# Order of the moved columns, weight sums and operand splits in a fused conv and FFN kernel

## The reference, cut to what matters

```python
x = x + L0_ffn(L0_cond(x, cond_128, conv weight, c_weight, bias), W, b, A, B, gate_w, gate_b)
x = x + L1_ffn(L1_cond(x, cond_128, W0..W2, weight, bias_k), W_base, b_base, router, lora_A, lora_B)
# L0_cond: grouped 9-tap convolution along the 1024 axis, plus a per-channel term
# L1_cond: a 64 x 64 channel mixture drawn per sample from 8 weights, plus a bias
# L*_ffn : x @ W.T + b, plus a rank-limited product chosen by a gate
```

## Time and profile before

| | us |
|---|---|
| median of 3 runs | 504.15 (504.13 to 504.69) |
| the profiled execution | 504.05 |
| its span, first to last instruction | 502.3 |
| TensorE busy in it | 493.3 (98%) |
| VectorE, GpSimd, ScalarE busy | 355.2, 160.6, 141.2 |

### The profile page before, as it was taken

The page is one execution under the profiler, slowest core; times in us unless marked ns, Lnnn a source line. Parts: engine busy times, 40 slices in busy tenths (PEclk is TensorE's granted clock), DMA queues, the critical chain, the costliest instruction groups (busy, mean ns, idle before and its releaser), DMA issues.

```text
span 502.3 us, 8338 instructions
## 1 busy us (share of the span) xinstructions
PE 493.3 (98%) x2889; PEld 456.3 (91%) x2889; DVE 355.2 (71%) x781; ACT 141.2 (28%) x298; POOL 160.6 (32%) x134
## 2 busy tenths in 40 slices
PE   8999999999999999999998999999999999999997
PEld 8989999999989899898997989898998989889886
DVE  4966998557495885958879668686666657657654
ACT  4732334242324323243152322121112112111200
POOL 1000020022455524555004744350626225062620
PEclk9999999999999999999999999999999999999999
DMA  8945205438286583867799863332515232160312
GB/s 312 327 143 173 86 1 158 147 116 281 68 277 216 199 275 108 275 206 222 247 412 404 331 196 119 127 105 71 202 44 188 85 126 106 64 209 2 126 43 84
DMA packets 43653, 86.40 MB, mean 172 GB/s; under 512 B 4299, under 2 KB 19259, under 8 KB 43612
## 3 DMA queue, kind: packets, MB, share of 16 engines
q1 hardware_dynamic: 34556, 63.49, 37.7%
q10 hardware_dynamic: 9056, 22.38, 12.2%
HBM read 58.81 MB, written 24.97 MB: 167 GB/s over the span
## 4 chain that ended last, share of the span: by engine, by line
PE 51%; DVE 2%; issue 0%; DVEq 0%
PE b_p L1729 6%; PE b_x L1749 4%; PE b_x L1748 4%; PE b_x L1746 4%; PE b_p L1730 3%; PE b_m L1705 3%; PE b_y L1749 3%; PE b_y L1746 3%; PE b_y L1748 3%; PE b_z L1748 2%; PE b_z L1749 2%; PE b_z L1746 2%; PE b_w L1749 1%; PE b_w L1748 1%; PE b_w L1746 1%; PE b_y L1705 1%
## 5 line engine op out<-in xcount | busy, mean ns | idle before, releaser
L730 ACT CAST a_hi<-mixed 128x512 fp32r<-128x512 f32 x63 | 37.7, 620 | 152.3 <-DVE mixed L1110 80.5
L655 POOL TENSOR_TENSOR xs<-xs,mixw_sb 128x512 f32<-128x512 f32 x28 | 38.3, 1379 | 118.4 <-DMA xs<-x_scratch 83.7
L1729 PE MATMUL b_p<-wp,a_hi 128*128 128x464 f32 (+1 forms) x224 | 72.6, 377 | 0.0
L1730 PE MATMUL b_p<-wp,a_lo 128*128 128x232 f32 (+1 forms) x224 | 60.1, 268 | 0.0
L1146 DVE TENSOR_TENSOR a_lo<-mixed,a_hi 128x512 fp32r<-128x512 f32 x63 | 53.4, 881 | 4.1 <-ACT a_hi L730 3.8
L1307 DVE TENSOR_TENSOR xs<-b_x,xs 128x464 f32<-128x464 f32 (+2 forms) x52 | 33.4, 642 | 27.7 <-PE b_x L1789 15.6
L741 ACT CAST s_hi<-s_sums 128x512 fp32r<-128x512 f32 x56 | 34.1, 620 | 59.8 <-POOL s_sums L618 36.1
L1154 DVE TENSOR_TENSOR s_lo<-s_sums,s_hi 128x512 fp32r<-128x512 f32 x56 | 43.9, 818 | 9.1 <-POOL s_sums L623 9.1
L1729 PEld LDWEIGHTS b_p<-wp,a_hi 128*128 128x128 f32 x224 | 42.1, 188 | 5.1
L618 POOL TENSOR_TENSOR s_sums<-mixed 128x512 f32<-128x512 f32 x13 | 17.9, 1376 | 80.6 <-DVE mixed L1107 55.5
L1730 PEld LDWEIGHTS b_p<-wp,a_lo 128*128 128x128 f32 x224 | 42.8, 191 | 0.6
(11 more groups left out here) (310 smaller groups left out, 1272.5 us busy)
## 6 DMA issues: line engine op xcount, KB each, us to landing
blk<-x_scratch SPq DMA_DIRECT2D x16, 512.0 KB, 4.0
xs<-in_x SPq DMA_DIRECT2D x30, 256.0 KB, 3.4
x_scratch<-xs SPq DMA_DIRECT2D x30, 256.0 KB, 3.8
xs<-x_scratch SPq DMA_DIRECT2D x28, 256.0 KB, 2.9
out_dram<-xs SPq DMA_DIRECT2D x27, 256.0 KB, 2.3
blk<-in_xblk SPq DMA_DIRECT2D x10, 516.0 KB, 3.7
w_raw<-in_wcat SPq DMA_DIRECT2D x8, 546.0 KB, 8.6
praw<-in_wcat ACTq DMA_DIRECT2D x8, 464.0 KB, 4.8
```

Source lines behind the costliest of these rows:

```text
L655: pool.tensor_tensor(x_rows, x_rows, bbase[:, a:b], ALU.add).then_inc(x_biased[q], 1)
L730: act.copy(a_hi[:, op, :, :], mixed[:, op, :, :]).then_inc(ahi_done[op], 1)
L1729: pe.matmul(both, x_hi, wp[:, k, :, 0:PLAIN[l]], start=(k == 0), stop=False, skip_group_check=True)
L1730: ins = pe.matmul(dst, x_lo, wp_hi[:, k, 0:PLAIN[l]], start=False, stop=(k == NCH - 1), skip_group_check=True)
```

## The change

Five edits, all in the order of work. The instructions are the same and none is added.

1. SyncE (`shift_pair` part of its list): `move_z(a, 0)` is issued ahead of the waits for the stores of pair g-1 and the loads of regions 3 and 1, not after them.
2. GpSimd: in pairs 3 to 6 the two `add_z` stand ahead of `prep(g)`, not after it.
3. ScalarE, pairs 3 to 6: `split_a(A11)`, `split_a(A12)` of the next pair ahead of all four `prep_split`.
4. VectorE, pairs 3 to 6: `split_a(A11)` and `split_a(A12)` right behind `take_first`; P5 taken after `fin11`; `prep_split` of blocks 0, 1 and 3 ahead of taking P6; `split_s(S4)`, `prep_split(2)`, the second `sum_mix` and the taking of `b_w` after it; `take_plain(0)` then.
5. Pair 7: `split_plain` ahead of `load_slot(T1, P5)` on ScalarE and ahead of taking P5 on VectorE.

```diff
@@ SyncE, shift pairs @@
+                    move_z(a, 0)
                     stored(3, g - 1)
                     load_x(3, g)
                     stored(1, g - 1)
                     load_x(1, g)
-                    move_z(a, 0)
                     if shifted(a - 2):
                         stored(2, g - 1)
                         load_x(2, g)
@@ GpSimd @@
             for g in range(FULL, LAST + 1):
-                if PREP_FIRST <= g <= PREP_LAST:
-                    prep(g)
                 if shifted(2 * g + 2):
                     add_z(2 * g + 2, 0)
                     add_z(2 * g + 2, 1)
+                if PREP_FIRST <= g <= PREP_LAST:
+                    prep(g)
@@ ScalarE, shift_pair @@
-                prep_split(0, g)
-                prep_split(1, g)
                 split_s(S4, g)
-                prep_split(3, g)
-                prep_split(2, g)
                 split_a(A11, g + 1)
                 split_a(A12, g + 1)
+                for part in (0, 1, 3, 2):
+                    prep_split(part, g)
                 prep_store(g)
@@ ScalarE, g == PAIRS - 1 @@
                     load_slot(T4, P4)
+                    split_plain()
                     load_slot(T1, P5)
-                    split_plain()
@@ VectorE, shift_pair @@
                 take_first(g)
-                dve.wait_ge(p_done[P5], made(g))
-                take(b_y, 3, g, took_p5)
+                split_a(A11, g + 1)
+                split_a(A12, g + 1)
                 sum_mix(b, 0)
                 dve.wait_ge(c11_done, g + 1)
                 dve.wait_ge(took_p1, made(g))
                 take(b_z, 0, g, fin11, BANK)
-                prep_split(0, g)
-                prep_split(1, g)
+                dve.wait_ge(p_done[P5], made(g))
+                take(b_y, 3, g, took_p5)
+                for part in (0, 1, 3):
+                    prep_split(part, g)
                 dve.wait_ge(p_done[P6], made(g))
                 take(b_x, 1, g, took_u2)
+                split_s(S4, g)
+                prep_split(2, g)
+                sum_mix(b, 1)
+                dve.wait_ge(c21_done, g + 1)
+                take(b_w, 2, g, took_w, BANK)
                 dve.wait_ge(fin11, g + 1)
                 dve.wait_ge(took_u2, made(g))
                 take_plain(0, g)
-                split_s(S4, g)
-                sum_mix(b, 1)
-                prep_split(3, g)
-                prep_split(2, g)
-                split_a(A11, g + 1)
-                dve.wait_ge(c21_done, g + 1)
-                take(b_w, 2, g, took_w, BANK)
                 dve.wait_ge(p_done[P7], made(g))
                 dve.wait_ge(took_w, made(g))
                 take(b_x, 2, g, fin21)
-                split_a(A12, g + 1)
                 split_a(A21, g + 1)
@@ VectorE, pair loop @@
+                if g == PAIRS - 1:
+                    split_plain()
                 dve.wait_ge(p_done[P5], made(g))
                 take(b_y, 3, g, took_p5)
...
                 if g == PAIRS - 1:
-                    split_plain()
                     split_slot(B11, 0)
                     split_slot(B11, 1)
```

## The result

| us | before | after |
|---|---|---|
| median of 6 runs | 504.66 (504.13 to 506.76) | 513.89 (512.33 to 516.11) |
| the profiled execution | 504.05 | 514.52 |
| its span | 502.3 | 512.8 |
| TensorE busy | 493.3 | 497.6 |

The ratio is 1.018 (1.015 to 1.021): slower, and by 9.2 us in the medians, where 4.8 were forecast for the span. The sign was right, the size was not; the median lies above the range.

A forecast was written before the change was run, and what follows sets the result against it. TensorE, busy 98% of the span at full clock, bounds the kernel, so only its gaps count. Span 502.3 + 6.0 (pairs 3 to 6) - 1.2 (pair 7) = 507.1, giving 508.9 us; range 505.6 to 512.6.

The forecast's parts named there:

- The sign and the chain: Pairs 3 to 6: late weight sums delay VectorE's prep_split, taking P6 and so P7; slower, +1.5 us a pair, chance 0.89.
- the new wait before the convolution: Pairs 3 to 6: TensorE waits 1.2 us for fin11 before the b_z convolution, contained in the 2.6 lost at P7.
- Faster: Rival: weight sums made by 166.9 don't decide, nothing new stalls, the five old stalls go: 498.6 us, chance 0.07.
- no change: Rival: only the 1.2 us fin11 stall shows and the P6 chain is hidden: 503.4 us, chance 0.04.
- The old stall's price: TensorE's wait before the b_x low-rank product loses 1.08 us in each of pairs 3 to 6, 1.47 in pair 7.
- The second move: Pair 4: 4.3 us from first issue to add; second add begins about 162.0, ends 163.3 instead of 164.5, 1.2 gained.
- The heavier rival: Three 256 KB loads ahead in the queue land the second move as late as before: 512.5 to 513.7 us, chance 0.11.
- The sums: GpSimd's weight sums in pair 4 can't start before 163.3; beside two VectorE splits they were taken to end at 169.3.
- P7 in the forecast's terms: Pair 4: P7 starts at 171.8 and not 169.21, 2.6 us lost, in each of pairs 3 to 6.
- The clock: Rival: a whole gap of 2.6 drops TensorE to 1.2 GHz, P7 takes 2.4 us more: above 518, chance 0.02.
- the later store of region 0: SyncE's store of region 0, made later by the new order: listed as covered and costed at nothing.
- the covered edits: Later prep_store and region 0 store, three loads behind move_z(0), ScalarE's prep_split casts, A21 and A22 splits: all costed at nothing.

The follow-up runs named there:

- the sums' move alone: Kernel before with only GpSimd's swap in pairs 3 to 6, both adds of moved columns ahead of the four weight sums: 519.23 us, ratio 1.028.
- taking it out with nothing in its place: Kernel before with VectorE's four prep_split right behind take_first and A11, A12 split behind fin11, in pairs 3 to 6: 499.79 us, ratio 0.9895.
- The plain weights' edit by itself: Kernel before with only split_plain of pair 7 ahead of load_slot(T1, P5) on ScalarE and of taking P5 on VectorE: 505.27 us, ratio 1.003.
- the moves' edit: Kernel before with only SyncE's move_z(a, 0) ahead of the two stores and loads: 504.66 us, ratio 0.9991.
- the kernel without the plain weights' edit: Kernel after with split_plain of pair 7 back in its old place, all other edits kept: 515.16 us, ratio 1.0215.

## Why the prediction was right or wrong

- *The sign and the chain: right.* The old wait went in all five places, the new wait before the convolution stands in all four pairs and that before P7 in pairs 3 and 6 (in 4 and 5 the convolution, slowed by the clock, fills its place), VectorE idles for the last sum before its first `prep_split` (0.67 in pair 4), and the sums' move alone makes the pairs longer. Faster and no change fell.
- *The old stall's price: right.* 1.08 a pair; taking it out with nothing in its place gave 1.18.
- *The second move: mis-sized.* "4.3 us" from first issue to add came from pair 4 alone. After, the four pairs took 5.3, 5.0, 6.2 and 4.9, and before itself had shown 5.1 and 5.8 in pairs 3 and 5 (4.3 in pair 6): TensorE's offsets repeat from pair to pair, the moves' don't. In pair 4 the first issue was 0.4 later than put too. So the second add ended 18.46, 19.55, 19.83 and 19.13 into the pair; 18.44 was forecast for all, which only pair 3 met. Against before, the add starts 0.12 sooner in pair 4 (18.27 for 18.39) and 0.2 in pair 3, and not 1.2; in pairs 5 and 6, which had been later in before, 1.1 and 1.3. Summed over four pairs the add ends 3.2 later than forecast. The heavier rival, with a chance of 0.11, had it as late as before, which is what pairs 3 and 4 show; that the loads ahead in the queue are the reason is not shown.
- *The sums: 5.6 for 6.0.* 165.65 to 171.27, a little better than the count by whole instructions (6.1), and at the 5.7 of before. Each of the two sums beside the splits was stretched by 0.3 to 0.4 and the two splits by 1.3. By the exclusive lock of the Trainium skill (SBUF — State Buffer, "SBUF: two separate sides") the instructions take turns, and the stretched ones agree with that; my count had given the sums the whole length of both splits, and the trace shows 0.8 of 1.2. From the end of the second add to P7 it takes 8.0 in each pair (8.02, 8.00, 7.99, 8.01), where 8.5 was forecast (26.94 - 18.44): 2.0 less in four pairs.
- *P7 in the forecast's terms.* It started 26.48, 27.55, 27.82 and 27.14 into the pairs, and 26.94 was forecast: 11.6 lost for 10.4, 1.2 more over four pairs. This is small by luck: the add's 3.2 too late and the chain's 2.0 too short go against each other, and the forecast had both wrong.
- *The clock: a rival with too small a chance and too high a price.* It stood at 0.02 and 2.4 us a pair, above 518 in all. I had taken from gaps of 0.92 to 1.31 that the new ones would leave the clock at full speed. They became 1.84 and 2.13 before the convolution, and each of these two was followed by a fall to 1.2 GHz. The convolution's loss was hidden, P6 being late anyway; the rest of P7 cost 0.58 each time (2.70 = 3.20 - 1.08 + 0.58 in pair 4, 2.97 = 3.47 - 1.08 + 0.58 in pair 5): 1.2. Together with the last point this is the 2.4 between 6.0 and 8.45. The six executions of after bear the clock out: three with a mean granted clock of 1.000 took 512.33 to 513.27, three with 0.993 to 0.996 took 514.52 to 516.11. So the clock alone doesn't explain the miss: even at full clock after is about 4 us above the forecast.
- *The step that failed: what lies behind pair 7, costed at nothing.* The sum ends with pair 7, and pairs 8 and 9 cost 3.11, the largest part of the miss. I had put "the later store of region 0" among the covered edits without naming what hides it. SyncE's list behind it holds the next 512 KB load, and in pair 6 both were put off towards the stretch where the loads of layer 1's weights fill the DMA engines (share 1.0). By the profiles it cost 1.44 in pair 9 by itself (0.9 by the medians, and 0.4 a shift pair through VectorE), and 2.1 of the 3.1 in pairs 8 and 9 went when it was moved back (a gain of 1.7 in all by the medians, not clear of noise). The plain weights' edit by itself costs 0.65 in pair 8 and 1.46 in pair 9 too, though in pair 7 it gives what was forecast: 1.35 for 1.2. The wait for `agg` in pair 8 stands only in kernels with that edit, so the 0.58 there goes with it. How the two share the 2.5 of pair 9 stays open, as pair 9 lost 1.25 in a profile of the moves' edit too, whose median did not change: the chain stands at an edge, 0.16 us from a wait in the profile of before.

In sum: 4.8 forecast; +1.2 from P7's start (+3.2 for the move, -2.0 for the chain behind it), +1.2 from the clock, +3.1 at the turn, +0.2 ahead of pair 3 and 0.15 less for pair 7 make 10.3, with the rounding of the terms the 10.5 of the profiled span. By the medians the change costs 9.2, and the miss is 5.0 (513.89 for 508.9) and not 5.7.

## What to carry to other kernels

An engine's idle time ahead of a slow transfer is the place for work whose inputs are there; a change that moves ready work behind the transfer makes that transfer's jitter part of the path, four times here, while filling the idle time with it won 1%. Before a store is costed at nothing, read what stands behind it in its queue in the last repetition, where the next phase's loads begin, and not only in the typical one. And a duration of a transfer is to be read from every repetition that the trace has, since the one that was read had been among the shortest of four (4.3, with others up to 5.8).

## What was not expected of the hardware

- The granted clock fell to 1.2 GHz after idle gaps of 1.84 and 2.13 us of TensorE, but not after gaps of 2.44 (pair 9, after) or 2.51 (pair 5 of the kernel without the plain weights' edit). The length of a gap alone does not tell it: in the kernel with the sums' move alone the same gap of 2.17 before the low-rank product stands four times, the clock fell behind the first and the last (at 147.03 and 251.49) and stayed full behind the two between. Window of after behind the second fall (the same columns):

```profile
204.00:208.00 4.00, 3.57 (x19) 2.90 (x19) 3.34 (x7) 1.16 (x2) 1.36 (x2) 0.72 0.00 0
208.00:212.00 4.00, 4.00 (x18) 3.78 (x19) 3.61 (x8) 1.95 (x4) 2.14 (x2) 0.86 0.53 192
```

- Two stores of 256 KB issued 2.4 us into pair 8 had landed only 22 us later, when the load that waits for them went out (276.92 to 298.88), and 18.8 later in before (269.66 to 288.43). In the same stretch, at about 400 GB/s, the loads of weights took 12.8 to 18.9 us to land.
